# Attention with a gated recurrence on one core: other places for v's projection and for the maxima matmuls in TensorE's program

## The reference

```
qkv = xn @ W_qkv + b_qkv                       # 16 heads of 64
scores = q @ k.T                               # per batch and head, 512 x 512
attention = softmax(scores / sqrt(64), axis=3)
attn = (attention @ v) @ W_out + b_out

for t in 0..7:                                 # xn[t] is 512 x 128
    f = sigmoid(xn[t] @ wf.T + c @ uf.T + bf)  # i likewise
    g = tanh(xn[t] @ wc.T + c @ uc.T + bc)
    c = f * c + i * g
h = tanh(xn @ wo.T + c @ uo.T + bo)

out = data + attn + h
```

## Time and profile before

| what | value |
|---|---|
| median of three executions | 908.32 us |
| the profiled execution | 911.83 us, span 910.0 us |
| TensorE matmul busy | 875.1 us (96%) |
| TensorE weight load busy | 554.0 us (61%) |
| VectorE busy | 571.1 us (63%) |
| GpSimd busy | 548.2 us (60%) |
| ScalarE busy | 444.7 us (49%) |
| TensorE on the chain that ended last | 89% |

### The profile page before, as it was taken

How to read it: one execution, slowest core, us unless ns; L and a number is a source line. 1 busy time by engine, 2 the same in 40 slices (tenths; PEclk the granted TensorE clock), 3 DMA queues, 4 the chain that set the end, 5 groups by cost and what they waited for, 6 DMA issues and landing times.

```text
span 910.0 us, 14933 instructions
## 1 busy us (share of the span) xinstructions
PE 875.1 (96%) x5429; PEld 554.0 (61%) x5429; DVE 571.1 (63%) x770; ACT 444.7 (49%) x579; POOL 548.2 (60%) x270
## 2 busy tenths in 40 slices
PE   4779999999999999999999999999999999999988
PEld 3545655655666666665666566665666566666643
DVE  6856666664766556665667476664766476665632
ACT  4335645652555555552555455552555355553531
POOL 4024644644777667773777677773777577774764
PEclk9669999999999999999999999999999999999999
DMA  7000000000100000000100000000100000000000
GB/s 232 1 0 1 9 17 0 1 13 1 36 2 13 0 1 34 0 12 0 35 0 12 0 23 12 0 12 0 35 0 12 0 23 12 0 13 1 13 13 12
DMA packets 18635, 13.75 MB, mean 15 GB/s; under 512 B 1298, under 2 KB 16176, under 8 KB 18608
## 3 DMA queue, kind: packets, MB, share of 16 engines
q1 hardware_dynamic: 18608, 13.39, 4.7%
HBM read 6.83 MB, written 2.10 MB: 10 GB/s over the span
## 4 chain that ended last, share of the span: by engine, by line
PE 89%; DVE 6%; ACT 2%; DMA 1%; issue 1%; SPq 1%; DVEq 0%
PE st L747 20%; PE pv L761 12%; PE misc L761 12%; PE st L689 9%; PE mx L728 8%; PE st L753 6%; PE mx L777 6%; PE mx L771 6%; PE pv L689 2%; DVE NM L507 2%; PE misc L673 2%; PE misc L689 2%; DMA probs<-in_L_attn_data_dram 1%; ACT probs L360 1%; DVE KL L493 1%; PE pv L673 1%
## 5 line engine op out<-in xcount | busy, mean ns | idle before, releaser
L507 DVE TENSOR_REDUCE NM<-mx 128x2 f32<-128x1024 f32 x256 | 313.8, 1226 | 172.7 <-PE mx L728 172.7
L360 ACT ACTIVATE probs<-st 128x1024 f32<-128x1024 f32 x256 | 257.3, 1027 | 93.9 <-PE st L753 88.7
L251 POOL TENSOR_TENSOR AT<-AT,RD 128x512 f32<-128x512 f32 x63 | 80.8, 1282 | 231.9 <-DVE RD L525 171.1
L259 POOL TENSOR_TENSOR PSUMK<-probs 128x1024 f32<-128x1024 f32 x64 | 153.4, 2397 | 99.5 <-ACT probs L360 99.5
L265 POOL TENSOR_TENSOR PSUMK<-PSUMK,probs 128x1024 f32<-128x1024 f32 x64 | 152.9, 2389 | 6.1
L272 POOL TENSOR_TENSOR PSUMK<-PSUMK,probs 128x1024 f32<-128x1024 f32 x64 | 152.8, 2387 | 6.1
L761 PE MATMUL misc<-probs,VALL 128*64 128x512 f32 x512 | 129.1, 593 | 0.9 <-DVE DL L472 0.9
L761 PE MATMUL pv<-probs,VALL 128*64 128x512 f32 x512 | 124.8, 607 | 0.7 <-DVE RES L478 0.7
L728 PE MATMUL mx<-KH,QH 64*128 64x512 f32 x512 | 112.4, 435 | 9.8 <-DVE NM L507 8.8
L747 PE MATMUL st<-QH,KH 64*128 64x512 f32 x512 | 107.4, 415 | 0.8 <-ACT probs L360 0.6
L747 PE MATMUL st<-QL,KH 64*128 64x512 f32 x512 | 101.5, 392 | 0.0
(11 more groups left out here) (179 smaller groups left out, 1240.5 us busy)
## 6 DMA issues: line engine op xcount, KB each, us to landing
probs<-in_L_attn_data_dram SPq DMA_DIRECT2D x4, 512.0 KB, 7.6
XSH<-XH SPq DMA_DIRECT2D x8, 256.0 KB, 2.4
XSL<-XL SPq DMA_DIRECT2D x8, 256.0 KB, 2.4
RES<-in_L_attn_data_dram SPq DMA_DIRECT2D x8, 256.0 KB, 2.8
out_dram<-RES SPq DMA_DIRECT2D x8, 256.0 KB, 2.3
probs<-in_L_attn_W_qkv_dram SPq DMA_DIRECT2D x3, 512.0 KB, 4.7
MROW<-TM SPq DMA_DIRECT2D x64, 4.0 KB
WO<-in_L_attn_W_out_dram SPq DMA_DIRECT2D x1, 512.0 KB, 4.8
```

The costliest lines, as they stand in the source:

```text
L251: nc.gpsimd.tensor_tensor(AT[:, s % PAIRS, :], AT[:, s % PAIRS, :], RD[:, s % 2, :], ALU.mult).then_inc(norm_done, 1)
L259: nc.gpsimd.tensor_tensor(PSUMK[:, s % 2, :, :], e[:, :, 0, :], e[:, :, 1, :], ALU.add).then_inc(sum_part, 1)
L360: nc.scalar.activation(probs[:, s % 2, :, u, :], st[:, u % 2, :, :], ACT.Exp, scale=SCALE).then_inc(exp_done, 1)
L507: nc.vector.tensor_reduce(NM[:, 0:4 * TB].rearrange("p (h a b) -> p h a b", h=2, a=2)[:, :, s % 2, b], mx[:, :, :], AX.X, ALU.max, negate= ...
```

## The change

`project_values` and `project_pair` now take a list of slots, 0 to 5, so that a call can issue one, two or three of the six. Each waits for its banks before slot 0 and for its first half before slot 3. The slots of v's projection are then issued one at a time between the score blocks of the loop's steps and of the last batch's, and M2 to M6 stand at other places among them; in the loop M7 is where it was, and M0 and M1 too. The matmuls, their operands and their number stay the same. In batch 0 the order up to P0 is as before; behind it two slots of P1 come ahead of M6.

```diff
-            def pair_of_halves(groups, swap, done):
+            def pair_of_halves(groups, slots, halved, done):
-                for i in range(3):
+                for slot in slots:
+                    swap, i = slot // 3, slot % 3
                     for h in range(2):
                         dst, terms = groups[h ^ swap]
...
-            def project_pair(s, k, swap):
+            def project_pair(s, k, t, slots):
...
+                if 0 in slots:
+                    pe.wait_ge(exp_done, 4 * t + 7 + k)
+                if 3 in slots:
+                    pe.wait_ge(p_half, 2 * t + 2 + 2 * k)
...
                     else:
+                        staged = 32 * n + 64
                         scores(n, t, s, 1)
                         if coming:
                             score_maxima(t + 2, s + 2, 1)
                         if ahead:
-                            wait(pe, pv_evac, t)
-                            project_values(1 if j < 2 else 0, 2 * (j % 2), 0, n, j)
+                            project_values(t, j, (0,), staged)
                         scores(n, t, s, 2)
+                        scores(n, t, s, 3, (0, 1))
                         if coming:
                             score_maxima(t + 2, s + 2, 2)
-                        scores(n, t, s, 3)
-                        scores(n, t + 1, s + 1, 0, (0, 1))
+                        if ahead:
+                            project_values(t, j, (1,), staged)
+                        scores(n, t, s, 3, (2, 3))
+                        scores(n, t + 1, s + 1, 0)
                         if coming:
                             score_maxima(t + 2, s + 2, 3)
-                        scores(n, t + 1, s + 1, 0, (2, 3))
+                        if ahead:
+                            project_values(t, j, (2,), staged)
                         scores(n, t + 1, s + 1, 1)
+                        scores(n, t + 1, s + 1, 2, (0, 1))
                         if coming:
                             score_maxima(t + 3, s + 3, 0)
-                        scores(n, t + 1, s + 1, 2)
-                        scores(n, t + 1, s + 1, 3, (0, 1, 2))
+                        scores(n, t + 1, s + 1, 2, (2, 3))
+                        if ahead:
+                            project_values(t, j, (3,), staged)
+                        scores(n, t + 1, s + 1, 3)
                         if coming:
                             score_maxima(t + 3, s + 3, 1)
-                        scores(n, t + 1, s + 1, 3, (3,))
-                        if ahead:
-                            project_values(1 if j < 2 else 0, 2 * (j % 2), 1, n, j)
                     if ahead:
-                        pe.wait_ge(exp_done, 4 * t + 7)
-                        project_pair(s + 4, 0, 0)
+                        project_pair(s + 4, 0, t, (0, 1, 2))
+                        if not first:
+                            project_values(t, j, (4, 5), 0)
+                        project_pair(s + 5, 1, t, (0, 1))
                     if coming:
                         score_maxima(t + 3, s + 3, 2)
                     if ahead:
-                        pe.wait_ge(exp_done, 4 * t + 8)
-                        project_pair(s + 5, 1, 0)
-                        pe.wait_ge(p_half, 4 * (STRETCHES * n + j) + 2)
-                        project_pair(s + 4, 0, 1)
-                        pe.wait_ge(p_half, 4 * (STRETCHES * n + j) + 4)
-                        project_pair(s + 5, 1, 1)
+                        project_pair(s + 5, 1, t, (2,))
+                        project_pair(s + 4, 0, t, (3, 4, 5))
+                        project_pair(s + 5, 1, t, (3, 4, 5))
                     if coming:
                         score_maxima(t + 3, s + 3, 3)
```

More of the change, by code:

```diff
@@ L688, in pair_of_halves @@
                         stationary, moving = terms[i]
-                        last = nc.tensor.matmul(dst, stationary[OWN[h], :], moving[OWN[h], :], start=(swap == 0 and i == 0),
-                                                stop=(swap == 1 and i == 2))
-                        if i == 2:
+                        last = nc.tensor.matmul(dst, stationary[OWN[h], :], moving[OWN[h], :], start=(slot == 0),
+                                                stop=(slot == 5))
+                        if slot == 2:
+                            last.then_inc(halved, 1)
+                        if slot == 5:
                             last.then_inc(done[h ^ swap], 1)
-            def project_pair(s, k, swap):
+            def project_pair(s, k, t, slots):
                 groups = []
@@ L699, in project_pair, with project_values @@
                     groups.append((dst, [(WH[:, c], XSH), (WL[:, c], XSH), (WH[:, c], XSL)]))
[L700 to L707, removed]
+                if 0 in slots:
+                    pe.wait_ge(exp_done, 4 * t + 7 + k)
+                if 3 in slots:
+                    pe.wait_ge(p_half, 2 * t + 2 + 2 * k)
+                pair_of_halves(groups, slots, p_half, (q_done, k_done))
+            def project_values(t, j, slots, staged):
+                half, tb = 1 if j < 2 else 0, 2 * (j % 2)
                 c = slice(2 * DIM + half * L, 2 * DIM + (half + 1) * L)
@@ L712, in project_values @@
                     groups.append((value_banks[k], [(XSH[:, b], WH[:, c]), (XSL[:, b], WH[:, c]), (XSH[:, b], WL[:, c])]))
-                pair_of_halves(groups, swap, (v_done, v_done) if swap else (v_half, v_half))
+                if 0 in slots:
+                    wait(pe, pv_evac, t)
+                    if j == 2:
+                        pe.wait_ge(d_xs, staged)
+                if 3 in slots:
+                    pe.wait_ge(v_half, t + 2)
+                pair_of_halves(groups, slots, v_half, (v_done, v_done))
             def project_v(half, tb, hi=XSH, lo=XSL, dst=misc):
@@ L866, in step @@
                         scores(n, t, s, 1, (3,))
-                        wait(pe, pv_evac, t)
-                        project_values(1 if j < 2 else 0, 2 * (j % 2), 0, n, j)
+                        project_values(t, j, (0, 1, 2), 64)
                         scores(n, t, s, 2, (0, 1))
@@ L871, in step @@
                         scores(n, t, s, 2, (2, 3))
-                        project_values(1 if j < 2 else 0, 2 * (j % 2), 1, n, j)
+                        project_values(t, j, (3, 4, 5), 0)
                         scores(n, t, s, 3, (0, 1))
```

## The result

The changed kernel took a median of 901.57 us over five executions (900.09 to 903.46), the kernel before 909.62 over five (907.50 to 911.11): a ratio of 0.9914 (95% interval 0.9892 to 0.9936), faster by 0.9%. Timed once more later, on the same chip as another variant: 900.74 us, ratio 0.9905 (0.9890 to 0.9919). Forecast was 898.7 us, in a range from 893.5 to 904.0. The profiled execution is the one of 901.57 us, span 899.8.

A forecast was written before the change was run, and what follows sets the result against it. TensorE, 96% busy, and what holds it up were taken as the bound. Loop and last-batch steps -10.4 us, batch 0 +0.8, sum -9.6, laid on the 908.32 us median: 898.7 us, range 893.5 to 904.

The forecast's parts named there:

- two rings, of 1.63 and 1.83 us: TensorE's loop steps: exponentials' ring needs 1.63 us (7.1 slots of 0.23), maxima's 1.83 (8.0); edit makes them 7 and 8.
- the whole gain lies ahead of M7: Second half of a loop step: all hangs on M7 and moves with it, nothing gives the 0.40 us back.
- The loop's steps: Loop's 24 steps and the last batch's first two: 0.40 us gained each, 26 x 0.40 = 10.4 us.
- no distance above 0.27: Sign of being right: in the loop's steps, distances of 0.31 to 0.34 us between score slots gone, none exceeding 0.27.
- Batch 0: Batch 0's four steps: M6 takes its own slot behind P1's wait, 0.2 us longer each, 0.8 us; bounds 0 to 2.
- The third step of the last batch: Last batch's step without projections, M5, M6, M7 one behind another: M ring unchanged, given 0.
- The waits' total: Sign of being right: weight loads' waits for reductions and exponentials fall by some 10 us.
- Waits that each show a whole load: Rival: eight exponential waits per loop step cost 0.13 us each; 16.7 us slower, 925 us; chance 0.05.
- No gain: Rival: maxima rings need 0.05 us more, or a cover behind M7 is false; about 908 to 909 us; chance 0.08.
- half: Rival: small waits scatter, each ring of seven pays 0.05 us; gain 0.2 a step, 904 us; chance 0.10.
- More: Rival: steps on a 0.23 us grid or better, batch 0 loss swallowed; 14.0 us gained, 894.3 us; chance 0.17.
- the scattered hundredths: Loop step, outside the five late starts: distances one or two hundredths too long; half of them, 0.06 us, counted as gained.

The follow-up runs named there:

- two half edits: Changed kernel with v's projection back in two blocks of three slots: 915.9 us, ratio 1.0063; changed kernel with M2 to M6 put back: 916.0 us, ratio 1.0064.
- The reordered waits: Changed kernel with ScalarE's wait for the scores written behind the waits for pv_done and sum_done: 900.46 us in one execution.
- the order was restored: Changed kernel with M6 ahead of all slots of P1 in batch 0 alone: 903.38 us in one execution; batch 0's j = 2 step 33.68 us.
- the four with the holes filled: Changed kernel with products with v between M5, M6, M7 of the last batch: 897.9 us; with further edits added: 896.6, 896.1, 896.1 us.
- the variant with filled holes: Changed kernel with batch 0's M6 ahead of P1, filled third and fourth last-batch steps, ScalarE's waits reordered in the loop alone: 896.1 us, ratio 0.9846.

## Why the prediction was right

**The mechanism.** That two rings, of 1.63 and 1.83 us, count in slots of 0.23, and that the edit makes one seven and the other eight slots long, held. The two half edits show it best, since they come out slower than the kernel before, by amounts forecast from the slot counts: 915 to 916 and 914 to 915 us were forecast, 915.9 and 916.0 measured, the second 1 us above its range. That the whole gain lies ahead of M7 held as well. From M7 to the end of the step it was 9.26 us in the earlier trace rows (487.09 to 496.35), and it is 9.26 in the changed kernel (483.61 to 492.87).

**The loop's steps: right kind, a little too large.** 0.40 us a step was taken; measured are 0.37 (9.5 us over 26). The steps j = 1, 2 and 3 gave 0.39, 0.36 and 0.43. The step j = 0 gave only 0.28, since there a 0.14 us later exponential met a ring that now had no room, and a stop of 0.05 + 0.10 came up before S2. The prediction counted all 26 steps alike and took the exponential's start from the one step of the earlier trace rows, which is a j = 3. The trace of the kernel before already had the late one: in the j = 0 step that follows, the exponential of S0 starts at 497.95, 0.57 behind its last slot at 497.38. The prediction's sentence that no distance above 0.27 would be left fails in this place (0.28 and 0.33). Before, S0 and S2 were nine slots apart, and that hid it. The reordered waits gave 0.13 of it back.

**Batch 0: right.** 0.8 us forecast, 4 x 0.2 measured (33.68 to 33.89), and gone when the order was restored.

**The third step of the last batch: right by its own account.** It was given 0. With the drop of the clock in both, it took 24.13 us before and 24.17 after; the 1.6 us of difference between the first two profiles are the clock.

**The waits' total: wrong.** I wrote that the weight loads' waits would fall by some 10 us, as the lost time does. They fell by 3: from 30.2 + 24.7 + 0.7 to 15.5 + 28.8 + 8.0. A load takes 0.11 us of a slot of 0.23, so a load can wait 0.1 us or so for nothing; the changed kernel has many such waits. The sum of waits on PEld is no measure of loss, the distance between starts is.

**The rivals.** Waits that each show a whole load are out. A small wait costs its lateness: 0.02 at S4 in the changed kernel, 0.03 at S5 in the earlier trace rows. A large one costs the lateness and the load together, which the need of 1.63 already holds. "No gain" and "half" are out by the median and by the steps. "More" is out as well: batch 0's loss was not swallowed, the step j = 0 gave less, and the scattered hundredths stayed in part (13.00 us for 56 distances, 12.88 on the grid).

**The median.** The measured 901.6 us are 2.9 above the forecast of 898.7. Of these, 1.3 are the kernel before, whose median came to 909.6 with five executions where 908.3 had been taken from three, and 1.6 are the gain, 8.0 for 9.6. Against the later 900.7 the gain is 9.1, from 909.9.

## What to carry to other kernels

Where an engine without idle time hands its results to others through one or two buffers, each buffer is a ring: add up, start to start, the own operation, the other engine's start, its length and the restart with its weight load, and divide by the engine's step. That number of whole steps must stand between the two uses; a need just above it (7.1 steps with 7 between, here) costs only the few hundredths that are missing. Several rings through the same stream have to be met at once, and an edit that serves one alone can cost more than none. When a ring is cut to fit to hundredths, look at every place where it occurs: a wait carried by a separate instruction (0.57 us instead of 0.43 here), harmless before, becomes the bound.

## What the hardware showed that was not expected

- Holes on TensorE were followed by a drop of its clock. Around M5 to M7 of the last batch it was busy for 1.58 of 4 us. Windows of the kernel before:

```profile
864.00:868.00 4.00, 1.58 (x10) 0.68 (x8) 2.45 (x2) 1.58 (x2) 3.86 (x3) 0.95 0.00 0
868.00:872.00 4.00, 4.00 (x15) 1.46 (x15) 1.41 (x2) 0.00 (x0) 3.86 (x2) 0.62 0.00 0
```

  The clock is at half (1.2 of 2.4 GHz) from 867.6 to 871.0. Of the seven profiles of kernels with these holes six have such a drop, 3.4 us long in five, 6.8 in one, at a cost of 1.6 and 3.0 us; of the four with the holes filled, all by the same edit, none has. Why the seventh has none stays open. On one chip, nine executions of the kernel before spread from 908.16 to 911.97 us, five of the changed kernel from 899.72 to 902.16 and five of the variant with filled holes from 894.66 to 896.30. That the drop is a part of the spread is likely, not shown; the start of the kernel adds a spread of its own.
- The same kernel's start differs by 3.3 us between two executions with different clocks. Windows of the changed kernel's first profile, and of its second:

```profile
39.90:46.80 6.90, 5.06 (x12) 2.57 (x12) 4.72 (x6) 2.60 (x5) 0.00 (x0) 0.50 0.00 0
```

```profile
39.90:46.80 6.90, 3.20 (x14) 1.61 (x12) 6.75 (x9) 3.30 (x5) 0.00 (x0) 0.99 0.00 0
```

  In the first profile the clock was at half from 27.9 to 62.1 us. In the second it was full in the stretch shown, and again from 57.0 on. The first scores started at 56.71 us in the one and 54.57 in the other, 2.1 us apart, and the second step of batch 0 at 92.6 and 89.3: the rest of the lead came between 57.0 and 62.1.
